# Batch-axis softmax attention: reciprocals moved from VectorE to ScalarE, and two of eight shifts written by ScalarE instead of by identity products

## What is computed

```python
Q = (x @ Wq.T + bq).reshape(B, S, H, dk)      # B = 32, S = 256, H = 16, dk = 8
K = (x @ Wk.T + bk).reshape(B, S, H, dk)
V = (x @ Wv.T + bv).reshape(B, S, H, dk)
scores = jnp.einsum('bqhd,bkhd->hbqk', Q, K)
attn = jax.nn.softmax(scores, axis=1)          # over the batch
heads = jnp.einsum('hbqk,bkhd->bqhd', attn, V).reshape(B, S, dm)
```

## Time and profile before

| | before |
|---|---|
| runs, us | 1595.75, 1589.63, 1594.35 |
| median of the runs, us | 1594.35 |
| span of the profiled execution, us | 1588.9 |
| busy share of the span: PE, DVE, ACT, POOL | 88%, 70%, 46%, 66% |
| attention of the first layer, first to last exponential, us from the span's start | 131.2 to 772.3 |

### The profile page before, as it was taken

One profiled execution on the slowest core, in us unless ns is written; L12 is line 12 of the kernel. 1 busy time (PEld: TensorE's weight loads), 2 busy tenths in 40 slices (PEclk: granted clock), 3 DMA queues, 4 the chain that ended last, 5 costly groups with the idle time before them and its releaser, 6 DMA issues. The chain is left out here.

```text
span 1588.9 us, 41679 instructions
## 1 busy us (share of the span) xinstructions
PE 1391.6 (88%) x14844; PEld 1079.3 (68%) x14845; DVE 1119.5 (70%) x1911; ACT 725.7 (46%) x1565; POOL 1043.7 (66%) x763
## 2 busy tenths in 40 slices
PE   6868999999999999999679995988999799999970
PEld 4635666666666666666469993776777599999960
DVE  5648999999999999999955563756754333333329
ACT  7824555555555555555334442643434244444430
POOL 6724888888888888888924444557777544444430
PEclk9969999999999999999799996999999899999995
DMA  6875233333333333331335442101111122222228
GB/s 218 281 221 149 63 86 88 88 88 88 88 88 88 88 84 84 82 86 29 122 104 181 143 126 87 41 30 44 58 41 46 39 68 66 65 67 65 66 74 288
DMA packets 112206, 155.17 MB, mean 98 GB/s; under 512 B 17856, under 2 KB 85696, under 8 KB 107200
## 3 DMA queue, kind: packets, MB, share of 16 engines
q1 hardware_dynamic: 78496, 106.64, 24.5%
q0 software_dynamic: 13344, 27.92, 5.3%
q10 hardware_dynamic: 20224, 18.65, 3.7%
HBM read 95.33 MB, written 57.82 MB: 96 GB/s over the span
## 5 line engine op out<-in xcount | busy, mean ns | idle before, releaser
L1002 POOL TENSOR_TENSOR V<-Ex,R 128x4096 f32<-128x4096 f32 x64 | 475.2, 7425 | 71.5 <-DVE R L854 71.4
L939 ACT ACTIVATE Ex<-pB 128x512 f32<-128x512 f32 x512 | 305.5, 597 | 264.1 <-PE pB L739 255.7
L832 DVE TENSOR_REDUCE mg<-pA 128x128 f32<-128x2048 f32 x128 | 288.8, 2256 | 8.4 <-PE pA L722 8.4
L848 DVE TENSOR_REDUCE Z<-Ex 128x64 f32<-128x2048 f32 x128 | 290.7, 2273 | 3.3 <-ACT Ex L939 3.1
L1087 POOL DMA_INDIRECT y_d<-x1yb,x1xb x136 | 131.8, 969 | 151.2 <-DVE x1yb L1224 144.7
L734 PE MATMUL pB<-mh,identb 128*128 128x512 bf16 x512 | 196.4, 384 | 0.2
L734 PE MATMUL pB<-ml,identb 128*128 128x512 bf16 x512 | 193.4, 378 | 0.0
L749 PE MATMUL pO<-V,Vh 128*8 128x128 f32 x4096 | 162.7, 280 | 13.5 <-POOL V L1002 13.5
L1764 POOL DMA_INDIRECT xs_d<-d_xn,d_idx x128 | 130.9, 1023 | 42.1 <-issue 35.3
L1224 DVE COPY x1yb<-x1pY 128x128 f32<-128x128 f32 x136 | 39.7, 292 | 160.8 <-PE x1pY L1121 160.7
L1110 PE MATMUL x1pU<-x1xT,x1w1s 128*128 128x128 f32 x1088 | 145.0, 276 | 0.2 <-ACT x1xT L1148 0.2
(11 more groups left out here) (265 smaller groups left out, 2530.2 us busy)
## 6 DMA issues: line engine op xcount, KB each, us to landing
w<-qs_d SPq DMA_DIRECT2D x48, 192.0 KB
w<-ks_d SPq DMA_DIRECT2D x48, 192.0 KB
qk<-qs_d SPq DMA_DIRECT2D x48, 192.0 KB
qk<-ks_d SPq DMA_DIRECT2D x48, 192.0 KB
x1xb<-xs_d SPq DMA_DIRECT2D x136, 64.5 KB, 1.8
f_ye<-y_d SPq DMA_DIRECT2D x16, 512.0 KB, 4.9
qs_d<-parts SPq DMA_DIRECT2D x16, 384.0 KB, 2.9
ks_d<-parts SPq DMA_DIRECT2D x16, 384.0 KB, 3.2
```

The source lines that it names most:

```text
L832: dve.tensor_reduce(mg[:, :, g], pA[:].rearrange("p b q -> p q b"), AX.X, ALU.max).then_inc(b_red, 1)
L848: dve.tensor_reduce(Z[:, q], Ex[:, j, q, :], AX.X, ALU.add).then_inc(b_sum, 1)
L939: act.activation(Ex[:, j, :, BG * g:BG * (g + 1)], pB[:, g % 2, :, :].rearrange("p b q -> p q b"), ACT.Exp).then_inc(b_exp, 1)
L1002: pool.tensor_tensor(En[:, j % 2, :, :].rearrange("p b q -> p q b"), Ex[:, j, :, :], R[:, j % 2, :].unsqueeze(2).broadcast_to([P, P, B]), ...
```

## The change

The reciprocal of the sums leaves VectorE. ScalarE computes it as exp(-ln Z): a Ln in place on Z and an Exp with scale -1 into R, for unit u - 2, behind exponential 1 of unit u; for the last two units, behind the whole sweep. Z is doubled. A table set that has Exp and Ln is loaded ahead of the sweep.

In groups 0 and 4 of every unit but the first, TensorE's two identity products go. ScalarE copies the negated maximum nm, in fp32 and broadcast over four batch elements, into the group's bank of pB: for group 4 behind exponential 3, for group 0 behind exponential 7 of the unit before. TensorE's score products of these groups wait for that copy (b_pre) and add to it. mh and ml are still made, for the other six groups. `unit_max` waits also for the shift of group 4 of four units ago, since it overwrites nm.

```diff
--- before.py
+++ after.py
@@ -586,7 +586,7 @@
             En = V[:].rearrange("p h n d -> p (h n d)").rearrange("p (s b q) -> p s b q", s=2, b=B)
             mh = sb("mh", [P, 4, P], BF16, ph)
             ml = sb("ml", [P, 4, P], BF16, ph)
-            Z = sb("Z", [P, P], F32, ph)
+            Z = sb("Z", [P, 2, P], F32, ph)
             R = sb("R", [P, 2, P], F32, ph)
             Oev = sb("Oev", [P, 2, NBG, P], F32, ph)
 
@@ -619,7 +619,9 @@
             b_s2 = sem("b_s2")
             b_exp = sem("b_exp")
             b_sum = sem("b_sum")
+            b_ln = sem("b_ln")
             b_r = sem("b_r")
+            b_pre = sem("b_pre")
             b_norm = sem("b_norm")
             b_vh = [sem("b_vh0"), sem("b_vh1")]
             b_pv = sem("b_pv")
@@ -629,6 +631,16 @@
             b_idx = sem("b_idx")
             b_sc = [sem("b_sc0"), sem("b_sc1")]
             LOADS = 2 * NPART * 16
+            INV_AT = 1
+            PRE_AT = (0, 4)
+
+            def preset(u, g):
+
+                return u >= 1 and g in PRE_AT
+
+            def presets(u, g):
+
+                return len(PRE_AT) * (u - 1) + PRE_AT.index(g) + 1
 
             room = Ex[:, 0, :, :].rearrange("p q b -> p (q b)")[:, 0:3 * NB0 * E + E * NS * TOPK]
             pad_fill, pad_tags, pad_rows, pad_copies, pads_written, table_parts = blocks("r0", 0, rows0, T, xs0_d, eb0, bs0, NB0, room, ph)
@@ -728,12 +740,15 @@
                 def s2_group(n, s, j, g):
 
                     qh, kc = j // 2, j % 2
-                    if not isinstance(n, int) or n >= 2:
-                        pe.wait_ge(b_exp, n - 1)
-                    for i, m in enumerate((mh, ml)):
-                        nc.tensor.matmul(pB[:, g % 2, :, :], identb[:],
-                                         m[:, j, :].unsqueeze(1).broadcast_to([P, BG, P]),
-                                         start=(i == 0), stop=False, skip_group_check=True)
+                    if preset(n // NBG, g):
+                        pe.wait_ge(b_pre, presets(n // NBG, g))
+                    else:
+                        if n >= 2:
+                            pe.wait_ge(b_exp, n - 1)
+                        for i, m in enumerate((mh, ml)):
+                            nc.tensor.matmul(pB[:, g % 2, :, :], identb[:],
+                                             m[:, j, :].unsqueeze(1).broadcast_to([P, BG, P]),
+                                             start=(i == 0), stop=False, skip_group_check=True)
                     for c in range(BG):
                         tok = (BG * g + c) * P
                         ins = nc.tensor.matmul(pB[:, g % 2, c, :],
@@ -837,21 +852,17 @@
                     dve.wait_ge(b_red, NM * u + NM)
                     if u >= 4:
                         dve.wait_ge(b_m, u - 3)
+                    if u >= 5:
+                        dve.wait_ge(b_pre, presets(u - 4, PRE_AT[-1]))
                     dve.tensor_reduce(nm[:, j, :], mg[:], AX.X, ALU.max, negate=True).then_inc(b_nm, 1)
 
                 def half_sum(v, j, i):
 
                     dve.wait_ge(b_exp, NBG * v + NBG)
-                    if i == 0 and (not isinstance(v, int) or v >= 1):
-                        dve.wait_ge(b_r, v)
+                    if i == 0 and v >= 2:
+                        dve.wait_ge(b_r, v - 1)
                     q = slice(i * P // 2, (i + 1) * P // 2)
-                    dve.tensor_reduce(Z[:, q], Ex[:, j, q, :], AX.X, ALU.add).then_inc(b_sum, 1)
-
-                def inverse(v, j):
-                    dve.wait_ge(b_sum, 2 * v + 2)
-                    if not isinstance(v, int) or v >= 2:
-                        dve.wait_ge(b_norm, v - 1)
-                    dve.reciprocal(R[:, j % 2, :], Z[:]).then_inc(b_r, 1)
+                    dve.tensor_reduce(Z[:, j % 2, q], Ex[:, j, q, :], AX.X, ALU.add).then_inc(b_sum, 1)
 
                 def body(h, s):
                     for j in range(4):
@@ -869,7 +880,6 @@
                             unit_max(u + 2, (j + 2) % 4)
                         if summed:
                             half_sum(v, vj, 1)
-                            inverse(v, vj)
 
                 def choose_rows():
 
@@ -905,7 +915,6 @@
                 last = 4 * H - 1
                 half_sum(last, 3, 0)
                 half_sum(last, 3, 1)
-                inverse(last, 3)
                 dve.wait_ge(b_norm, 4 * H - 3)
                 for part in parts[1:]:
                     part()
@@ -928,6 +937,22 @@
                         act.wait_ge(b_od[qh], 16 * BG * h)
                     g = slice(half * NBG // 2, (half + 1) * NBG // 2)
                     act.copy(Oev[:, qh, g, :], pO[:, g, :]).then_inc(b_oev, 1)
+
+                def preset_shift(u, j, g):
+
+                    act.wait_ge(b_nm, u + 1)
+                    act.wait_ge(b_exp, NBG * u + g - 1)
+                    act.copy(pB[:, g % 2, :, :], nm[:, j, :].unsqueeze(1).broadcast_to([P, BG, P]))\
+                       .then_inc(b_pre, 1)
+
+                def inverse(v, j):
+
+                    act.wait_ge(b_sum, 2 * v + 2)
+                    act.activation(Z[:, j % 2, :], Z[:, j % 2, :], ACT.Ln).then_inc(b_ln, 1)
+                    if v >= 2:
+                        act.wait_ge(b_norm, v - 1)
+                    act.wait_ge(b_ln, v + 1)
+                    act.activation(R[:, j % 2, :], Z[:, j % 2, :], ACT.Exp, scale=-1.0).then_inc(b_r, 1)
 
                 def body(h, s):
                     for j in range(4):
@@ -939,6 +964,11 @@
                             act.activation(Ex[:, j, :, BG * g:BG * (g + 1)],
                                            pB[:, g % 2, :, :].rearrange("p b q -> p q b"),
                                            ACT.Exp).then_inc(b_exp, 1)
+                            nu, ng = (u, g + 1) if g + 1 < NBG else (u + 1, 0)
+                            if nu < 4 * H and preset(nu, ng):
+                                preset_shift(nu, nu % 4, ng)
+                            if g == INV_AT and u >= 2:
+                                inverse(u - 2, (j + 2) % 4)
                             if g == 5 and j % 2 == 0 and started(h, 1):
                                 evac(h - 1, j // 2, 0)
                             if g == 6 and (j < 2 or not is_last(h, H)):
@@ -961,9 +991,12 @@
                 act.wait_ge(b_qk[0][0], LOADS)
                 store_v(act, VPART * len(V_AT))
                 act.wait_ge(b_row, 1)
+                nc.scalar.preload_act_table_set("natural_log_exp_and_others")
                 high_part(0, 0)
                 high_part(1, 1)
                 sweep(H, body)
+                inverse(4 * H - 2, 2)
+                inverse(4 * H - 1, 3)
                 for qh in range(2):
                     evac(H - 1, qh, 0)
                     evac(H - 1, qh, 1)
```

## The result

The changed kernel takes 1537.5 us (median of four runs, 1535.9 to 1538.9) against 1592.8 for the kernel before, run beside it: a ratio of 0.9659, 95% interval 0.9642 to 0.9675. It is 55 us faster.

What follows compares the result with a forecast made beforehand. VectorE, 99.3% busy in the middle of the batch attention, was taken as the bound: 60 x (10.16 - 9.20) = 57.6 us, less 0.9 at the tail, gives 57, so 1594 - 57 = 1537 us; range 1529 to 1562.

Steps and rivals of the forecast that it cites:

- VectorE's round sets the pace: Middle of batch attention: VectorE's round falls from 10.17 to 9.17 us, taken as 9.20, over 60 units; forecast chance 0.73.
- The reciprocal is worth 1.00 us per unit: VectorE, half_sum to group_max: 3.18 us with the reciprocal between, 2.18 without, so 1.00 us saved per unit.
- TensorE at 8.8 us: TensorE's work per unit falls from about 9.7 to 8.8 us without the identity products of groups 0 and 4.
- GpSimd at 8.97 us: GpSimd's round of normalisation, scatter and low part: 10.16 less 1.19 us idle is 8.97, fitting under 9.17.
- ScalarE's prices: ScalarE's added work per unit: two shifts at 0.58 us, Ln and Exp at 0.30 each, 1.76 us in all.
- The round by way of the shift of group 4: Second round crossing ScalarE, through exponentials, Ln, Exp and that shift to TensorE: put at 8.6 us.
- The shift of group 0: First round crossing ScalarE: shift ends 1.31 us after unit_max, round 8.7 us, TensorE waits up to 0.4 us.
- The third round: The reciprocal reaching GpSimd by way of ScalarE: 17.8 us over two units, so 8.9 us each.
- Ends: Run-in and tail: added table load costs nothing, later normalisations at the tail cost 0.9 us against the gain.
- ScalarE was not within a tenth of setting the pace: First rival, ScalarE sets the pace: second round 9.3 us gives 1544, 9.6 us gives 1561; chance 0.15.
- The slower rival: Ln and Exp don't stay in one table: two 1.28 us loads per unit, 11.2 us round, 1657 us; chance 0.07.
- The third rival, no change: Something off these engines, above all loads of queries and keys, takes the gain back: 1590 or so; chance 0.05.

Runs made afterwards that it cites:

- after_again: The changed kernel as it is, run again on the same chip as min_of_two: 1538.1 us.
- after_third: The changed kernel as it is, run again on the same chip as the run with sums in three pieces: 1535.8 us, ratio 0.9668.
- dve_extra: Changed kernel with one more 128x256 to 128x128 reduction on VectorE per unit, ahead of unit_max: 1556.9 us.
- recip_only: Changed kernel without its shifts: reciprocals on ScalarE, all eight groups with identity products again: 1561.6 us, ratio 0.982 to the kernel before.
- four_shifts: Changed kernel with shifts by ScalarE in groups 0, 2, 4 and 6 instead of 0 and 4: 1555.9 us.
- act_chain4: Changed kernel with four more 128x128 copies on ScalarE behind each unit's Exp, each waiting for the one before: 1554.6 us.
- act_extra3: Changed kernel with three more 128x128 copies on ScalarE behind each unit's Exp, not waiting for each other: 1536.0 us.
- shifts_1_5: Changed kernel with the two shifts in groups 1 and 5 in place of 0 and 4: 1701.8 us.
- tables: Changed kernel with two table loads in every unit, one ahead of Ln and one behind Exp: 1720.9 us.
- min_of_two: Changed kernel with group_max negating and unit_max an elementwise minimum of the two halves' results on VectorE: 1682.2 us, ratio 1.0567 to the kernel before.
- shift_only: Changed kernel with the reciprocals back on VectorE, the two shifts by ScalarE kept: 1588.5 us, ratio 0.9993 to the kernel before.

## Why the prediction was right, point by point

**VectorE's round sets the pace.** Right. 9.17 us had been worked out and 9.20 taken; 9.23 is measured, and from 145.01 to 691.05, the first group_max of units 2 and 61, 59 units take 9.26 us each, one wait of 1.04 us for TensorE among them. The profiles of after_again and after_third have no such wait and 9.24 us each. The 0.06 us over 9.17 is mostly VectorE's own: the first group_max takes 2.28 us instead of 2.23 and the next operation starts 2.19 us behind it instead of 2.15. dve_extra shows that there is no other bound in front.

**The reciprocal is worth 1.00 us per unit.** Right in its term, 2.19 us from half_sum to group_max. recip_only shows that only 0.47 us of it comes out while TensorE's round is 9.69.

**TensorE at 8.8 us.** Right: a half without a wait takes 4.41 us, 8.82 a unit, and the shift of group 0 fills the rest with its 0.42 us; up to 0.4 had been forecast. Some expectations above took 9.0 (9.23 less the 0.25 us of the profile), which counts too little of the wait. The 9.69 us of recip_only, 8.82 and twice 0.44, and the 9.34 of four_shifts, 8.82 and twice 0.26, bear the 8.8 out.

**GpSimd at 8.97 us.** Right: it waits 14.0 us for R between 160 and 680 us, some 56 units, 0.25 each, so 8.98.

**ScalarE's prices.** 0.58 and 0.30 were taken, 0.59, 0.30 and 0.31 measured. That a shift into PSUM might cost under 0.58 us does not show: it takes 0.59 us, the copy out of PSUM 0.58. The round by way of the shift of group 4 was put at 8.6, and act_chain4 gives 8.4. The shift of group 0 ends 412.60 + 0.59 = 413.19, 1.32 us behind unit_max's end at 411.87; 1.31 had been taken. The third round, 8.9 us by way of the reciprocal, was lengthened by no run, so its size stays an estimate.

**Ends.** 0.9 us had been set against the gain; the last normalisation starts 37.4 us behind the first group_max of unit 61 where it was 36.7, so 0.7. Between the first queued transfer of ScalarE's stage and that last normalisation the profiles show 684.0 and 630.1 us, 53.9 less; the spans differ by 53.6. Ahead of that stretch the changed kernel is 2.2 us sooner and behind it 2.5 us later, where nothing was changed.

**Luck.** That 1537 was met to half a microsecond is luck in part. The gain was 55 us, not 57, as the round is 9.23 us and not 9.20; and the base it was taken from, 1594.35, the median of three runs, lies 1.55 us over the 1592.8 of the four.

**Rivals.** ScalarE was not within a tenth of setting the pace: act_extra3 swallows 0.6 us. The slower rival had its mechanism right and its price too small, 1657 against 1721: the term left out was the clock that TensorE loses in this run, where it waits 2 us a round, 67 us. The change keeps its table: four loads in the whole span against three. The third rival, no change, falls with the 55 us, and the DMA engines stay at 38%.

## What to carry to other kernels

When the busiest engine has no gaps, write down the round of every engine, and of every path that crosses engines, before shortening it; here five rounds lay within 0.8 us, and each half of the change brought half of the gain or none without the other. An operation moved to another engine is free where the waiting engine has work of its own to do meanwhile: the same two shifts gain 24 us behind a group of TensorE products and lose 164 us one group later. Ahead of giving VectorE a second SBUF input, look at what GpSimd is reading.

## What the runs showed of the hardware that was not expected

A two-input operation of VectorE (128x128, minimum) stood still until GpSimd's 7.4 us multiply had ended. Its 64 executions take 0.29 us at the least, which is what had been estimated and is what the four take that meet no multiply of this kind, 2.25 us in the median and 2.80 at the most.

TensorE's granted clock did not stay at full, 2.4 GHz, in the runs with long waits in each round. In shifts_1_5 (1.2 us for the shift), tables (2.1 us) and min_of_two (up to 2.9 us) it fell to half in some rounds and not in others, with means over 100 us of 0.95 to 0.97, 0.85 to 0.93 and 0.87 to 0.89 between 200 and 600 us. In act_chain4 (0.5 us), in the changed kernel (0.25 us) and in shift_only (0.8 us for the shift and 0.35 us for group_max) it stayed at 1.00. So in the first three runs a wait of TensorE cost more than its length: some 25 us of the 164 in shifts_1_5, some 67 in tables.
